# First attention: the products of probabilities and values issued for four steps at once in place of two

## Chip, cores, metric

One Trainium2 chip, one core in use. The metric is the time of the whole program on the device in microseconds (us), the median of several runs. The kernel before takes 1048.2 us, the median of 3 runs (1046.62 to 1052.95).

## What is computed

The program is a chain of cross-attention layers L0 to L3, each with its MLP, over 4 batches in float32. The change touches the attention of L0 alone, cut here to what matters (the queries come from 256 latent rows in each batch, the keys and values from 64 context rows joined with those 256 rows, 16 heads of 16):

```python
q = (latents @ q_w + q_b).reshape(b, 256, 16, 16)
kv = (concatenate([x, latents], axis=1) @ kv_w + kv_b).reshape(b, 320, 16, 16, 2)
kmat, v = kv[..., 0], kv[..., 1]
attn = einsum('bkhd,bnhd->bhkn', q, kmat) / 16
attn = softmax(where(mask, attn, -inf))
attn_out = einsum('bhkn,bnhd->bkhd', attn, v).reshape(b, 256, 256)
attn_out = attn_out @ out_w + out_b + latents
```

After it come an RMS norm and the MLP of L0, then the layers L1 to L3, which the change leaves alone.

## The kernel before

The first attention is `attend0` on PE (TensorE), with partner loops on ACT, DVE and POOL. It has N = 64 steps, one for each batch b (4), pair of heads r (8) and half u of the 256 query rows (2); `step0(n)` maps a step to them. Sixteen steps make one batch, called a block here, and "step s of a block" is i mod 16. The order on every engine is the written order of the loops, and each engine runs its own list; semaphores (`wait_ge`, `then_inc`) tie them together. There is no scheduler.

In iteration i of its loop PE issues, in this order: `scores(i)` (L592, two products of a head's queries and all keys, into one of two pairs of banks of `ps`); `spread(i + 4)` (L578, in even i also L581), which lays out keys or queries of a later pair of heads; `turn(i - 3)` (L603, five transposes of the normalised probabilities `prob0`, into banks 4 and 5 of `ps`, of which there is one set); in odd i from 5 on `values(i - 5)` (L616), for the steps i - 5 and i - 4. Each `values` call multiplies the 5 tiles of transposed probabilities `pT0` of its two steps with the values `V0`. `V0` has 32 columns, so the matmul uses a 128*32 part of the array, and the two steps of a call lie in different parts. After that come, in some steps of a block, extra work: `base` (L546, steps 8 and 12, projections of the next batch), `values_of` (L557, steps 10 and 14; L561 and L562, step 0) and `output` (L626, steps 4 and 6). A float32 matmul is two records in the trace, so the ten matmuls of a `values` call are the row "L616 x20".

The partners. DVE in iteration i: `max0(i)` (L1303, the row maximum of the scores, after `scores(i)`), `invert0(i - 1)` (L1318), in odd i `spread0(i + 4)` (L1295), in steps 9, 10, 13 and 14 `split0` (L1282 and L1284, SBUF to SBUF), and last `copy0(i - 3)` (L1309, the transposes out of `ps` into `pT0`, after `turn(i - 3)`). ACT: `spread0`, then `exp0(i)` (L1048) once the maximum is there, and `values0` (L1058) after every eighth step. POOL: the product of the probabilities with 1/sum (L441).

The two waits that the prediction follows are in `turn`: it waits for `pt0_ready`, that is for `copy0` of the step before, since the banks must be empty; and in `max0`, which waits for `scores`.

```python
pe.wait_ge(pt0_ready, n)              # turn(n): copy0(n - 1) is done
dve.wait_ge(s0_ps, n + 1)             # max0(n)
dve.wait_ge(t0_ps, n + 1)             # copy0(n)
```

Of the kernel before, what the change touches and what calls it, by code (L numbers as in the profile page):

```python
# [19 lines left out]
I32 = mybir.dt.int32  # L20
# [5 lines left out]
P = 128  # L26
D = 256
DH = D // P
B = 4
S = 256  # L30
C = 64
# [14 lines left out]
VT0 = 5  # L46
# [62 lines left out]
def build(nc, t):  # L109
    ctx = ExitStack()  # L110
    with ctx:
        def sb(name, shape, dt=F32):
            return ctx.enter_context(nc.sbuf_tensor(name, shape, dt))

        def sem(name):
            return ctx.enter_context(nc.semaphore(name))
# [8 lines left out]
        e16q = sb("e16q", [1, P])  # L125
        e48_f = sb("e48_f", [P, P])
        e48 = sb("e48", [P, P], F32R)
        mask_i = sb("mask_i", [P, B * C], I32)
        mask_u = sb("mask_u", [1, B * C], U8)
        mask_f = sb("mask_f", [P, B * C])  # L130
        mask0 = sb("mask0", [P, B * C], F32R)
        mask2 = sb("mask2", [1, B * C])
        arena = sb("arena", [P, 16384])
# [8 lines left out]
        V0 = arena[:, 5632:10752].rearrange("p (b t r c) -> p b t r c", b=B, t=VT0, r=PAIRS)  # L142
# [3 lines left out]
        prob0 = arena[:, 13824:13824 + 4 * 2 * KEYS0].rearrange("p (k n) -> p k n", k=4)  # L146

        copies_f = arena[:, 0:512].rearrange("p (w c n) -> p w c n", w=2, c=2)

        HL = sb("HL", [P, DH, 2, KEYS0 + S], F32R)  # L150

# [11 lines left out]
        u = sb("u", [P, 2, D])  # L163
# [22 lines left out]
        neg_half = sb("neg_half", [P, 2])  # L186
        sq = sb("sq", [P, D + 1])
        PN = H * C + H
        prob = sb("prob", [P, 2, PN])
        pT_all = sb("pT_all", [P, 4 * VT0 * P])  # L190
        pT = pT_all[:, 0:2 * 8 * P].rearrange("p (k c n) -> p k c n", k=2, c=8)
        pT0 = pT_all[:, :].rearrange("p (k c n) -> p k c n", k=4, c=VT0)
        mx = sb("mx", [P, 2, H])
        mx2 = sb("mx2", [P, 2, H])
        sm = sb("sm", [P, 2, H])
# [6 lines left out]
        ps = ctx.enter_context(nc.psum_tensor("ps", [P, 8, 512], F32))  # L202
# [27 lines left out]
        base_copied = sem("base_copied")  # L230
# [7 lines left out]
        pv0_ps = sem("pv0_ps")  # L238
# [4 lines left out]
        pt0_ready = sem("pt0_ready")  # L243
# [34 lines left out]
        rows_done = sem("rows_done")  # L278
# [18 lines left out]
        def col(name, i=0, n=1):  # L297
            at = COLS[name][0] + i
            return cols[:, at:at + n]
# [8 lines left out]
        def step0(n):  # L308

            quad, s = n // 4, n % 4  # L310
            return quad // 4, 2 * (quad % 4) + s % 2, s // 2
# [206 lines left out]
        def _(pe):  # L518
            mm = nc.tensor.matmul
# [18 lines left out]
            def attend0():  # L538
# [26 lines left out]
                def spread(n):  # L565

                    pair, w = n // 2, n % 2
                    b, r = pair // PAIRS, pair % PAIRS
                    m, j = r // 4, r % 4
                    cols_of = slice(KEYS0, KEYS0 + S) if w else slice(0, KEYS0)  # L570
                    width = S if w else KEYS0
                    if n >= 1:
                        pe.wait_ge(kq_ready, n)
                    if n >= 2 and w == 0:
                        pe.wait_ge(kq_dve, n // 2)
                    pe.wait_ge(hl_ready, 4 * b + 2 * m + w + 1)
                    for c in range(2):
                        last = mm(ps[:, 7, 0:width], copies[:, j, w, c, :], HL[:, m, c, cols_of],  # L578
                                  start=(c == 0), stop=(c == 1 and w == 1))
                    if w == 0:  # L580
                        last = mm(ps[:, 7, 0:C], e48[:, :], mask0[:, b * C:(b + 1) * C], start=False, stop=True)  # L581
                    last.then_inc(kq_ps, 1)

                def scores(n):
                    b, r, u = step0(n)
                    pair = b * PAIRS + r
                    pe.wait_ge(kq_ready, 2 * pair + 2)
                    pe.wait_ge(kq_dve, pair + 1)
                    if n >= 2:
                        pe.wait_ge(p0_ready, n - 1)  # L590
                    for e in range(2):
                        last = mm(ps[:, 2 * (n % 2) + e, 0:KEYS0], Q0[:, pair % 3, e, u * P:(u + 1) * P],  # L592
                                  K0[:, pair % 3, :], start=True, stop=True)
                    last.then_inc(s0_ps, 1)
# [11 lines left out]

                def values(n):

                    pe.wait_ge(pt0_ready, n + 2)
                    if n % 8 == 0 and n > 0:  # L610
                        pe.wait_ge(o0_ready, n // 8)
                    for c in range(VT0):
                        for i in (n, n + 1):
                            b, r, u = step0(i)
                            at = slice(32 * (r % 4), 32 * (r % 4) + 32)
                            last = mm(ps[at, 6, u * P:(u + 1) * P], V0[:, b, c, r, :], pT0[:, i % 4, c, :],  # L616
                                      start=(c == 0), stop=(c == VT0 - 1))
                    last.then_inc(pv0_ps, 1)

                def output(g):  # L620
# [19 lines left out]
                for i in range(N + 4):  # L640
                    step, b = i % 16, i // 16
                    if i < N:
                        scores(i)
                    if i + 4 < N:

                        if i == 1:
                            pe.wait_ge(base_copied, 3)
                        elif step in (9, 13) and b + 1 < B:
                            pe.wait_ge(base_copied, 4 * (b + 1) + (1 if step == 9 else 3))
                        spread(i + 4)  # L650
                    if 3 <= i < N + 3:
                        turn(i - 3)
                    if i >= 5 and i % 2 == 1:

                        if step == 1 and b < B:
                            pe.wait_ge(v0_ready, 3 * b + 3)
                        elif step in (5, 7) and b >= 1:
                            pe.wait_ge(rows_done, 2 * (b - 1) + (1 if step == 5 else 2))
                        elif step in (9, 13) and b + 1 < B:
                            pe.wait_ge(base_copied, 4 * (b + 1) + (2 if step == 9 else 4))  # L660
                        elif step in (11, 15) and b + 1 < B:
                            pe.wait_ge(v0_ready, 3 * (b + 1) + (1 if step == 11 else 2))
                        values(i - 5)

                    if i == 0 or step in (8, 12) and b + 1 < B:
                        if i == 8:
                            pe.wait_ge(in_kin, 16)
                        pe.wait_ge(kq_ready, i + 5)
                        base(2 if i == 0 else 4 * (b + 1) + (0 if step == 8 else 2))

                    if step == 0 and b < B:
                        if b == 0:
                            pe.wait_ge(base_copied, 2)
                        values_of(b, 2)
                    elif i == 2:
                        pe.wait_ge(v0_ready, 3)
                        base(3)
                    elif step in (4, 6) and 1 <= b < B:
                        output(2 * (b - 1) + (0 if step == 4 else 1))
                    elif step in (8, 12) and b + 1 < B:  # L680
                        if step == 12:
                            pe.wait_ge(o0_ready, 2 * b + 1)
                        base(4 * (b + 1) + (1 if step == 8 else 3))
                    elif step in (10, 14) and b + 1 < B:
                        values_of(b + 1, 0 if step == 10 else 1)
# [276 lines left out]

            pe.wait_ge(in_base, 32)
            attend0()
            mlp(0)
            keys(0, 0)
# [30 lines left out]
        def _(act):  # L997
# [54 lines left out]
            def values0(half):  # L1052

                b, d = half // 2, half % 2
                act.wait_ge(pv0_ps, 4 * (half + 1))
                if b >= 2 and d == 0:
                    act.wait_ge(o_ps, 2 * (b - 1))
                a_(oT0[:, b % 2, :, d, :], ps[:, 6, 0:2 * P].rearrange("p (u n) -> p u n", u=2), ACT.Identity,  # L1058
                   bias=col("L0_v_b", d)).then_inc(o0_ready, 1)
# [17 lines left out]
            for i in range(N + 4):  # L1077
                step, b = i % 16, i // 16
# [159 lines left out]
        def _(dve):  # L1238
            v = nc.vector
# [15 lines left out]
            for j in range(4):  # L1255
                last = v.tensor_scalar(copies[:, j, :, :, :], copies_f, col("strip", j), None, ALU.mult)
# [47 lines left out]

            def copy0(n):
                dve.wait_ge(t0_ps, n + 1)
                if n >= 4:
                    dve.wait_ge(pv0_ps, (n - 4) // 2 + 1)
                v.tensor_copy(pT0[:, n % 4, :, :].rearrange("p c n -> p (c n)"),  # L1309
                              ps[:, 4:6, :].rearrange("p q n -> p (q n)")[:, 0:VT0 * P]).then_inc(pt0_ready, 1)  # L1310

            def invert0(n):
# [16 lines left out]
            for i in range(N + 3):  # L1329
                step, b = i % 16, i // 16  # L1330
# [379 lines left out]
```

## Time and profile before

| what | value |
|---|---|
| median of 3 runs | 1048.2 us (1046.62 to 1052.95) |
| the profiled execution | 1048.33 us |
| its span, first to last instruction | 1046.5 us |
| mean granted TensorE clock | 0.983 |
| busy PE, PE weight loads, DVE, ACT, POOL | 958.0, 781.1, 631.1, 462.3, 344.7 us |

The profiled execution's own time is 1.8 us above its span. "Busy" counts the time in which an engine runs at least one instruction; it is an average over stages with different limits, and it doesn't say which engine sets the pace in the first attention. The granted clock is told in shares of 2.4 GHz, with 0.50 for 1.2 GHz.

### The profile page before, as it was taken

The page shows a single profiled execution, that of the slowest core. Times are in us where ns is not written, and L with a number is a line of the kernel's source. Part 1 is how long each engine was busy: PE and PEld are TensorE (multiplying, and loading weights), DVE is VectorE, ACT ScalarE, POOL GpSimd, SP SyncE. Part 2 cuts the span into 40 slices and gives each one's busy share as a digit, 9 for nine tenths or more (in the row PEclk, how much of TensorE's full clock was granted, in tenths as well). Part 3 has the DMA queues.
Part 4 walks back from the last instruction along what each step waited for, and adds up shares of the span by engine and source line. Part 5 has one row for each costly group of instructions (what it writes and reads, how often), then busy time and mean ns, then how long its engine had stood idle before and what let it go on. Part 6 is the DMA issues. An engine that isn't in the chain of part 4 may idle for free.

```text
span 1046.5 us, 15013 instructions
## 1 busy us (share of the span) xinstructions
PE 958.0 (92%) x5272; PEld 781.1 (75%) x5272; DVE 631.1 (60%) x1412; ACT 462.3 (44%) x1108; POOL 344.7 (33%) x382
## 2 busy tenths in 40 slices
PE   6789889799998999989799899799998989989898
PEld 4677778688895778856688688688885778756787
DVE  3788988611778847798611463511778847798410
ACT  3566667432564336633331342432673326633421
POOL 2644545410453325433321010110443335443210
PEclk8899999999999999999999998999999999999999
DMA  9100000000462004310000200200460004200000
GB/s 348 45 2 2 2 1 2 1 1 1 122 212 81 1 1 143 109 52 1 1 1 1 81 1 1 92 1 1 141 249 23 1 10 152 81 1 1 1 11 30
DMA packets 15020, 52.40 MB, mean 50 GB/s; under 512 B 1507, under 2 KB 4067, under 8 KB 13796
## 3 DMA queue, kind: packets, MB, share of 16 engines
q1 hardware_dynamic: 14948, 51.46, 14.4%
q8 instruction: 43, 0.70, 0.3%
q14 instruction: 29, 0.24, 0.1%
HBM read 50.41 MB, written 1.05 MB: 49 GB/s over the span
## 4 chain that ended last, share of the span: by engine, by line
PE 81%; DVE 11%; issue 3%; ACT 3%; POOL 1%; DMA 0%; SPq 0%; DVEq 0%; ACTq 0%
PE ps L947 11%; PE ps L771 10%; PE ps L795 9%; PE ps L934 9%; PE ps L698 5%; PE ps L700 5%; PE ps L738 5%; PE ps L727 4%; PE ps L616 4%; PE ps L603 3%; PE ps L783 2%; PE ps L592 2%; DVE pT_all L1309 2%; PE ps L841 2%; PE ps L546 1%
## 5 line engine op out<-in xcount | busy, mean ns | idle before, releaser
L771 PE MATMUL ps<-arena,hT 128*128 128x512 f32 x256 | 117.9, 604 | 15.0 <-ACT hT L1101 15.0
L795 PE MATMUL ps<-arena,pT_all 128*128 128x256 f32 x512 | 116.5, 381 | 7.5 <-ACT pT_all L1177 4.7
L1422 DVE TENSOR_TENSOR x<-ps,x 128x512 f32<-128x512 f32 x16 | 11.1, 692 | 183.9 <-PE ps L947 183.9
L934 PE MATMUL ps<-hT,w 128*128 128x256 f32 x512 | 114.8, 380 | 4.8 <-ACT hT L1120 4.8
L450 POOL TENSOR_TENSOR rstd<-var,neg_half 128x1 f32<-128x1 f32 (+1 forms) x56 | 36.4, 651 | 247.8 <-DVE var L1355 247.8
L947 PE MATMUL ps<-w,arena 128*128 128x256 f32 x512 | 113.3, 379 | 1.8 <-DVE x L1422 1.8
L441 POOL TENSOR_TENSOR arena<-arena,rinv 128x640 f32<-128x640 f32 x64 | 80.2, 1254 | 99.8 <-DVE rinv L1318 99.7
L795 PEld LDWEIGHTS ps<-arena,pT_all 128*128 128x128 f32 x512 | 94.7, 190 | 21.5 <-ACT pT_all L1177 5.7
L934 PEld LDWEIGHTS ps<-hT,w 128*128 128x128 f32 x512 | 96.0, 190 | 18.0 <-issue 5.6
L947 PEld LDWEIGHTS ps<-w,arena 128*128 128x128 f32 x512 | 97.1, 190 | 15.6 <-issue 2.5
L1131 ACT ACTIVATE arena<-ps,cols 128x256 f32<-128x256 f32 x128 | 53.6, 470 | 107.8 <-PE ps L934 107.8
L771 PEld LDWEIGHTS ps<-arena,hT 128*128 128x128 f32 x256 | 48.3, 192 | 65.7 <-issue 46.9
L469 POOL TENSOR_TENSOR prob<-prob,rinv 128x512 f32<-128x512 f32 x32 | 49.5, 1547 | 140.8 <-DVE rinv L1490 140.8
L1184 ACT ACTIVATE prob<-prob 128x512 f32<-128x512 f32 x32 | 20.2, 631 | 145.0 <-DVE prob L1480 145.0
L1048 ACT ACTIVATE arena<-ps,nb 128x320 f32<-128x320 f32 x128 | 66.3, 523 | 27.0 <-DVE nb L1303 24.9
L434 POOL TENSOR_TENSOR vacc<-vacc,vpart 128x256 f32<-128x256 f32 x60 | 44.1, 734 | 89.9 <-ACT vpart L1153 89.8
L1303 DVE TENSOR_REDUCE nb<-ps 128x2 f32<-128x640 f32 x64 | 52.4, 819 | 25.1 <-PE ps L592 25.0
L603 PE MATMUL ps<-ident,arena 128*128 128x128 f32 x320 | 47.9, 281 | 21.1 <-DVE pT_all L1309 21.0
L727 PE MATMUL ps<-HL,wq 128*128 128x256 f32 x384 | 67.2, 310 | 0.0
L425 POOL TENSOR_TENSOR u<-ring,lnb 128x256 f32<-128x256 f32 x64 | 66.3, 1036 | 0.0
L738 PE MATMUL ps<-ring,VT 128*128 128x256 f32 x256 | 66.0, 379 | 0.3 <-DVE x L1422 0.2
L700 PE MATMUL ps<-ctxT,ring 128*128 128x256 f32 x256 | 65.7, 379 | 0.0
(150 smaller groups left out, 1888.4 us busy)
## 6 DMA issues: line engine op xcount, KB each, us to landing
ring<-in_heads_dram SPq DMA_DIRECT2D x64, 512.5 KB, 3.6
w<-in_w_dram SPq DMA_DIRECT2D x8, 1024.0 KB, 7.3
x<-in_x_dram SPq DMA_DIRECT2D x1, 1024.0 KB, 10.2
lnb<-in_lnb_dram SPq DMA_DIRECT2D x4, 256.0 KB, 8.9
ring<-in_wp_dram SPq DMA_DIRECT2D x1, 1024.0 KB, 5.2
out_dram<-x SPq DMA_DIRECT2D x4, 256.0 KB, 2.1
arena<-in_kinT_dram SPq DMA_DIRECT2D x1, 960.0 KB, 7.5
brow<-in_brow_dram SPq DMA_DIRECT2D x1, 768.0 KB, 11.5
```

Source lines behind the costliest of these rows:

```text
L425: g.tensor_tensor(u[:, k, :], ring[:, n % RING, 512:768], scale, ALU.mult).then_inc(u_ready, 1)
L441: g.tensor_tensor(w, w, rinv[:, n % 2, 0:2].unsqueeze(2).broadcast_to([P, 2, KEYS0]), ALU.mult)\
L603: last = nc.tensor.transpose(ps[:, 4 + c // 4, (c % 4) * P:(c % 4 + 1) * P], prob0[:, n % 4, c * P:(c + 1) * P], ident[:, :])
L700: last = mm(ps[:, k, 256:512], w[:, 256 + d * P:256 + (d + 1) * P], ctxT[:, h % 2, d, :], start=(d == 0), stop=(d == 1))
L727: last = mm(ps[:, 2 + k, d * B * C:(d + 1) * B * C], wq[:, k, c, d * P:(d + 1) * P], KT[:, k, e, :], start=(p == 0), stop=(p == 2))
L738: last = mm(ps[:, 4 + k, g * D:(g + 1) * D], VT[:, k, g * P:(g + 1) * P], ring[:, n % RING, WO:WO + D], start=True, stop=True)
L771: last = mm(ps[:, half, :], hT[:, k, d, 0:P], A[:, d, b // 2, cols_of, sl, :].rearrange("p r s k -> p r (s k)"), start=(d == 0), stop=(d = ...
L795: last = mm(ps[:, 6, 0:D], pT[:, k, c, :], VW[:, b, c, :], start=(c == 0), stop=(c == PAIRS - 1))
L934: last = mm(ps[:, f // 2, (f % 2) * 256:(f % 2 + 1) * 256], w1[:, d, f * P:(f + 1) * P], hT[:, k, d, :], start=(d == 0), stop=(d == 1))
L947: last = mm(ps[:, 5 + u, 0:D], hid[:, k, f, u * P:(u + 1) * P], w2[:, f, :], start=(f == 0), stop=(f == FT - 1))
L1048: last = a_(prob0[:, n % 4, e * KEYS0:(e + 1) * KEYS0], ps[:, 2 * (n % 2) + e, 0:KEYS0], ACT.Exp, bias=nb[:, n % 2, e:e + 1], scale=-1.0, ...
L1131: a_(hid[:, b % 2, f, :], ps[:, f // 2, (f % 2) * 256:(f % 2 + 1) * 256], gelu, bias=col(bias, f)).then_inc(hid_ready, 1)
```

## The change

`values(n)` is now called in the iterations i = 7, 11, 15, ..., 67, for the steps i - 7 to i - 4, as two pairs in a row; before, it was called in every odd iteration from 5 on, for two steps. So a pair's products that stood in the steps 1, 5, 9 and 13 of a block stand two steps later, in front of those of steps 3, 7, 11 and 15. The transposed probabilities get eight slots in place of four, and the waits and counts follow (`pv0_ps` now counts groups of four). To make room in SBUF, `prob`, used by later stages, lies in `pT_all`, and `mask_i` and `mask_f`, used at the start, lie in `arena`; no instruction, size or order of theirs changes.

```diff
-        prob = sb("prob", [P, 2, PN])
-        pT_all = sb("pT_all", [P, 4 * VT0 * P])
+        pT_all = sb("pT_all", [P, 8 * VT0 * P])
+        prob = pT_all[:, 2 * 8 * P:2 * 8 * P + 2 * PN].rearrange("p (k n) -> p k n", k=2)
...
-        pT0 = pT_all[:, :].rearrange("p (k c n) -> p k c n", k=4, c=VT0)
+        pT0 = pT_all[:, :].rearrange("p (k c n) -> p k c n", k=8, c=VT0)
...
-                    pe.wait_ge(pt0_ready, n + 2)
+                    pe.wait_ge(pt0_ready, n + 4)
                     if n % 8 == 0 and n > 0:
                         pe.wait_ge(o0_ready, n // 8)
-                    for c in range(VT0):
-                        for i in (n, n + 1):
-                            b, r, u = step0(i)
-                            at = slice(32 * (r % 4), 32 * (r % 4) + 32)
-                            last = mm(ps[at, 6, u * P:(u + 1) * P], V0[:, b, c, r, :], pT0[:, i % 4, c, :],
-                                      start=(c == 0), stop=(c == VT0 - 1))
+                    for two in (n, n + 2):
+                        for c in range(VT0):
+                            for i in (two, two + 1):
+                                b, r, u = step0(i)
+                                at = slice(32 * (r % 4), 32 * (r % 4) + 32)
+                                last = mm(ps[at, 6, u * P:(u + 1) * P], V0[:, b, c, r, :], pT0[:, i % 8, c, :],
+                                          start=(c == 0), stop=(c == VT0 - 1))
                     last.then_inc(pv0_ps, 1)
...
-                    if i >= 5 and i % 2 == 1:
+                    if i >= 7 and i % 4 == 3:
 
-                        if step == 1 and b < B:
+                        if step == 3 and b < B:
                             pe.wait_ge(v0_ready, 3 * b + 3)
...
-                        values(i - 5)
+                        values(i - 7)
...
-                act.wait_ge(pv0_ps, 4 * (half + 1))
+                act.wait_ge(pv0_ps, 2 * (half + 1))
...
-                if n >= 4:
-                    dve.wait_ge(pv0_ps, (n - 4) // 2 + 1)
+                if n >= 8:
+                    dve.wait_ge(pv0_ps, (n - 8) // 4 + 1)
```

On PE, the steps 9 to 11 of the first block, where the trace of before waits most: `scores` is L592, `spread` L578 and L581, `turn` L603, `values` L616, `values_of` L557. Before:

```order
L592 MATMUL ps<-K,Q 128x320 x2
L578 MATMUL ps<-HL,copies 128x256 x2
L603 MATMUL ps<-ident,arena 128x128 x5
L616 MATMUL ps<-pT_all,arena 32x128 x10
L592 MATMUL ps<-K,Q 128x320 x2
L578 MATMUL ps<-HL,copies 128x320 x2
L581 MATMUL ps<-mask,e 128x64
L603 MATMUL ps<-ident,arena 128x128 x5
L557 MATMUL ps<-arena 128x128 x4
L592 MATMUL ps<-K,Q 128x320 x2
L578 MATMUL ps<-HL,copies 128x256 x2
L603 MATMUL ps<-ident,arena 128x128 x5
```

The same steps on PE in the changed kernel (its line numbers are higher by one or two, so `scores` is L593 and `values` L618), with the row that follows them:

```order
L593 MATMUL ps<-K,Q 128x320 x2
L579 MATMUL ps<-HL,copies 128x256 x2
L604 MATMUL ps<-ident,arena 128x128 x5
L593 MATMUL ps<-K,Q 128x320 x2
L579 MATMUL ps<-HL,copies 128x320 x2
L582 MATMUL ps<-mask,e 128x64
L604 MATMUL ps<-ident,arena 128x128 x5
L558 MATMUL ps<-arena 128x128 x4
L593 MATMUL ps<-K,Q 128x320 x2
L579 MATMUL ps<-HL,copies 128x256 x2
L604 MATMUL ps<-ident,arena 128x128 x5
L618 MATMUL ps<-pT_all,arena 32x128 x20
```

The ten products between the transposes of step 9 and the scores of step 10 are gone, and behind the transposes of step 11 stand twenty in place of ten. DVE, ACT and POOL keep their instructions and the order of these.

## Rows read from the trace of the kernel before

**Rows 1.** Windows: the first, second and fourth block; busy us of each engine, granted clock.

```profile
18.13:69.40 51.27, 41.12 (x306) 33.27 (x305) 38.17 (x65) 29.64 (x92) 24.40 (x23) 0.87 0.22 88
69.40:113.18 43.78, 38.99 (x362) 33.55 (x360) 37.47 (x67) 29.06 (x90) 20.05 (x17) 1.00 0.00 1
...
157.00:198.90 41.90, 36.41 (x375) 30.85 (x373) 34.21 (x67) 24.41 (x80) 21.54 (x19) 1.00 0.01 2
```

**Rows 2.** Waits of PE, 18 to 200 us: total us, times, longest us.

```profile
PE ps L603 <- DVE pT_all L1309: 21.0, 22, 2.1
```

**Rows 3.** Timeline of PE and DVE, steps 2 and 3 of the second block: start us, us.

```profile
73.87 0.56 PE L592 MATMUL ps<-K,Q 128*128 128x320 f32 x2
...
74.47 0.82 DVE L1303 TENSOR_REDUCE nb<-ps 128x2 f32<-128x640 f32 x1 [0.21 <-PE ps L592]
...
74.59 0.74 PE L603 MATMUL ps<-ident,arena 128*128 128x128 f32 x5
...
75.09 0.54 PE L592 MATMUL ps<-K,Q 128*128 128x320 f32 x2
...
75.41 0.80 DVE L1309 COPY pT_all<-ps 128x640 f32<-128x640 f32 x1
...
76.13 0.81 DVE L1303 TENSOR_REDUCE nb<-ps 128x2 f32<-128x640 f32 x1
...
76.36 0.74 PE L603 MATMUL ps<-ident,arena 128*128 128x128 f32 x5 [0.49 <-DVE pT_all L1309]
...
77.02 1.29 PE L616 MATMUL ps<-pT_all,arena 128*32 128x128 f32 x20
...
77.57 0.82 DVE L1309 COPY pT_all<-ps 128x640 f32<-128x640 f32 x1
...
78.24 0.56 PE L592 MATMUL ps<-K,Q 128*128 128x320 f32 x2
...
78.84 0.82 DVE L1303 TENSOR_REDUCE nb<-ps 128x2 f32<-128x640 f32 x1 [0.45 <-PE ps L592]
```

**Rows 4.** Timeline of PE from 77.38 us: what is left of that L616 group.

```profile
77.38 0.93 PE L616 MATMUL ps<-pT_all,arena 128*32 128x128 f32 x14
```

**Rows 5.** Timeline, steps 9 to 12 of the second block: PE, DVE and POOL.

```profile
91.96 1.29 PE L616 MATMUL ps<-pT_all,arena 128*32 128x128 f32 x20
92.26 1.25 POOL L441 TENSOR_TENSOR arena<-arena,rinv 128x640 f32<-128x640 f32 x1 [1.97 <-DVE rinv L1318]
...
92.74 0.96 DVE L1282 CAST HL<-arena 128x320 fp32r<-128x320 f32 x1
...
93.18 0.56 PE L592 MATMUL ps<-K,Q 128*128 128x320 f32 x2
...
93.87 0.19 PE L581 MATMUL ps<-mask,e 128*128 128x64 f32 x1
...
94.26 0.82 DVE L1309 COPY pT_all<-ps 128x640 f32<-128x640 f32 x1
...
95.23 0.74 PE L603 MATMUL ps<-ident,arena 128*128 128x128 f32 x5 [1.17 <-DVE pT_all L1309]
...
98.38 0.74 PE L603 MATMUL ps<-ident,arena 128*128 128x128 f32 x5 [0.98 <-DVE pT_all L1309]
```

**Rows 6.** Windows round the fall of the granted clock in the first block.

```profile
28.85:31.80 2.95, 1.09 (x6) 0.74 (x5) 2.45 (x7) 2.70 (x10) 2.59 (x3) 1.00 0.07 26
32.00:35.20 3.20, 1.50 (x7) 1.53 (x8) 2.49 (x5) 1.15 (x4) 2.04 (x3) 0.50 0.00 0
```

**Rows 7.** Timeline of PE, first block, steps 3 to 5, at the lower clock.

```profile
33.70 1.30 PE L603 MATMUL ps<-ident,arena 128*128 128x128 f32 x5 [2.09 <-DVE pT_all L1309]
34.65 0.88 PE L592 MATMUL ps<-K,Q 128*128 128x320 f32 x2
...
37.23 1.97 PE L616 MATMUL ps<-pT_all,arena 128*32 128x128 f32 x20
```

**Rows 8.** Timeline of PE, the last two turns and values of the attention.

```profile
194.68 1.29 PE L616 MATMUL ps<-pT_all,arena 128*32 128x128 f32 x20
195.89 0.77 PE L603 MATMUL ps<-ident,arena 128*128 128x128 f32 x5
197.57 1.29 PE L616 MATMUL ps<-pT_all,arena 128*32 128x128 f32 x20 [0.92 <-DVE pT_all L1309]
```

More of the change, by code:

```diff
@@ L127, in build @@
         e48 = sb("e48", [P, P], F32R)
-        mask_i = sb("mask_i", [P, B * C], I32)
         mask_u = sb("mask_u", [1, B * C], U8)
-        mask_f = sb("mask_f", [P, B * C])
         mask0 = sb("mask0", [P, B * C], F32R)
@@ L148, in build @@
         copies_f = arena[:, 0:512].rearrange("p (w c n) -> p w c n", w=2, c=2)
+        mask_i = arena[:, 512:768].bitcast(I32)
+        mask_f = arena[:, 768:1024]
         HL = sb("HL", [P, DH, 2, KEYS0 + S], F32R)
@@ L652, in attend0 @@
                         turn(i - 3)
-                    if i >= 5 and i % 2 == 1:
-                        if step == 1 and b < B:
+                    if i >= 7 and i % 4 == 3:
+                        if step == 3 and b < B:
                             pe.wait_ge(v0_ready, 3 * b + 3)
[L657 to L660, printed above, removed]
+                        elif step == 7 and b >= 1:
+                            pe.wait_ge(rows_done, 2 * b)
                         elif step in (11, 15) and b + 1 < B:
+                            pe.wait_ge(base_copied, 4 * (b + 1) + (2 if step == 11 else 4))
                             pe.wait_ge(v0_ready, 3 * (b + 1) + (1 if step == 11 else 2))
-                        values(i - 5)
+                        values(i - 7)
                     if i == 0 or step in (8, 12) and b + 1 < B:
@@ L1306, in copy0 @@
                 dve.wait_ge(t0_ps, n + 1)
-                if n >= 4:
-                    dve.wait_ge(pv0_ps, (n - 4) // 2 + 1)
-                v.tensor_copy(pT0[:, n % 4, :, :].rearrange("p c n -> p (c n)"),
+                if n >= 8:
+                    dve.wait_ge(pv0_ps, (n - 8) // 4 + 1)
+                v.tensor_copy(pT0[:, n % 8, :, :].rearrange("p c n -> p (c n)"),
                               ps[:, 4:6, :].rearrange("p q n -> p (q n)")[:, 0:VT0 * P]).then_inc(pt0_ready, 1)
```

## The prediction, made before the changed kernel had run

> **What bounds the kernel now.** I read first the windows of the blocks of sixteen steps [rows 1]: a full block takes 43.8 us (the third as well as the second), PE is busy for 39.0 of them and DVE for 37.5. Neither is clearly the bound; with two engines this close one has to ask who waits for whom, step by step. The waits of PE [rows 2] have one name in them: 22 times the transposes (L603, `turn`) wait for DVE's copy of the transposes of the step before (L1309), 21.0 us in all. So the banks of the transposes tie PE to DVE. The timeline of two neighbouring steps shows the loop [rows 3]. Even step: scores at 73.87, transposes at 74.59, next scores at 75.09, 1.22 us in all; PE is fast. Odd step: the scores have run ahead, but the transposes wait until 76.36, 0.15 after DVE's copy ends at 76.21; then come the values at 77.02, and the next scores at 78.24. DVE in turn starts its maximum 0.60 after the scores start (78.24 to 78.84) and had sat idle for 0.45. So PE waits for DVE in front of the odd transposes, and DVE waits for PE behind the odd values. In steps 9 to 12 [rows 5] both transposes wait, 1.17 and 0.98 us: DVE has the splits (L1282, L1284) in front of its copy.
>
> What matters for the change is where the values stand. Those at step 9 begin at 91.96 and are followed by scores at 93.18, and the transposes of step 10 begin only at 95.23, when DVE is ready. **The values of step 9 hide behind DVE; those of steps 3 and 11 stand behind a late transpose and in front of the scores, and hide behind nothing.** The change moves the first kind to the place of the second.
>
> **The price of a pair of steps in `values`.** The group is 20 records; 14 of them remain at 77.38 [rows 4], so six took 0.36 us, and the 14 take 0.79 up to the start of the last plus its own tail, some 0.057 each: 1.14 for twenty. From the start of the group to the next scores it is 1.22 (77.02 to 78.24), from transposes to values 0.66 (76.36 to 77.02) and from transposes straight to scores 0.50 (74.59 to 75.09). So a pair costs PE 0.66 + 1.22 - 0.50 = 1.38 where it stands alone, and 1.14 behind another. Sixteen joined groups save PE 16 x 0.24 = 3.8 us of its own time, which counts only where PE sets the pace.
>
> **Steps 9 to 12 and 13 to 16, six groups of four.** Without the values of step 9 the scores of step 10 come 1.38 earlier, at 91.80. That helps nobody: DVE's list up to the copy that ends at 95.08 (inversion, `spread0`, cast, difference, copy) rests on nothing that PE now does sooner. The cast at 92.74 takes 0.96 and ends 0.19 after POOL's product (92.26 + 1.25), and its place behind that product does not change. So the transposes stay at 95.23 and 98.38. Then come 40 records in place of 20: +1.14, uncovered. Six groups: 6 x 1.14 = **6.84**.
>
> **Plain groups of four.** Here DVE can recover something. I take two pairs like rows 3 and count from the first scores. Before: transposes 0.72 and 2.49, next scores 4.37, and the same again, 8.74 in all. After: the first transposes are the same; the second pair's scores come at 2.49 + 0.50 = 2.99. The copy that starts at 77.57 - 73.87 = 3.70 and takes 0.82 ends at 4.52, so the third transposes start at 4.67 (before 5.09). DVE's next maximum follows its copy by 0.72 (75.41 to 76.13), at 4.42; its copy follows that by 0.94 (74.47 to 75.41), at 5.36, but not before the transposes are done (0.82 after their start, 74.59 to 75.41), at 5.49; it ends at 6.29. Fourth transposes 6.44, values 7.10, next scores 7.10 + 1.22 + 1.14 = 9.46. That is +0.72: of 1.14 moved, 0.42 is caught up. The steps 0 to 3 and 4 to 7 of the last three blocks (six groups) hold extra PE work in even steps (L561, L626), so they lie between 0.72 and 1.14; taking the same recurrence through them with that work gives some 0.95: 6 x 0.95 = **5.7**. The one group without it (steps 8 to 11 of the last block): **0.72**. The next group has no `spread`, so DVE is shorter and catches up more: **0.45**.
>
> **The two ends.** First group, steps 4 to 7: the values of step 5 ran at 1.2 GHz for part of their 1.97 us [rows 7] and go to step 7, where the clock was 2.4 GHz; what is saved and what is added cancel, **+0.15**, from -0.5 to +2. Last group [rows 8]: the values at 194.68 stood where the next transposes followed at once, but each transposition there has a copy to wait for of 1.0 us, so little is gained; both pairs now come last, behind the last copy, with ACT's `values0`, the outputs and the norm waiting: **+1.14**.
>
> Edits at nothing: the new waits of `values`, for `pt0_ready` n + 4, ask for the same copy that `turn` of that iteration has already waited for; the `pv0_ps` wait of `copy0` asks for a group that was issued before and was never late; `prob`, `mask_i`, `mask_f` move in memory only. ACT's `values0` waits 1.14 longer in every eighth step, with nothing queued behind it that is due before PE's next step.
>
> **The sum.** 0.15 + 6.84 + 5.7 + 0.72 + 0.45 + 1.14 = **15.0 us**, for all sixteen joined groups. Bounds by the same rows: 16 x 0.72 = 11.5 and 16 x 1.14 = 18.2. All of it lies ahead of the L0 MLP, which can't begin before the last outputs, and the later stages only shift.
>
> **The granted clock** comes on top. It fell once in this attention: after 28.85, where PE was busy for 1.09 of 2.95 us, it went from 1.00 to 0.50, 1.2 GHz [rows 6]. The changed kernel makes a new hole: after step 10's mask matmul, which ended at 94.06 and now ends at 92.7, PE does nothing up to 95.23, 2.5 us in place of 1.17, six times over, and there are three waits of about 1.0 in a row at the end. At the lower clock the transposes take 1.30 for 0.74 and the scores 0.88 for 0.56 [rows 3, 7]; with the work of `values_of` and `spread` slowed alike, and the 0.98 of the next wait as cover, a fall costs about 1.3, and up to 3 if it reaches the joined values. I take three falls of 1.3, **4 us**; the ends are none (0) and seven of 3 (21).
>
> Against the profiled execution (1048.33, 0.1 from the median) that is 1048.2 + 15 + 4 = **1067**.
>
> **Rivals.** *Faster: PE is the bound.* If the 0.24 per joined group were gained in full and DVE followed, the time would be 1048.2 - 3.8 = 1044. For it: PE is the busiest engine. Against: PE's 22 waits in rows 2, and the values of step 9, which nobody waits for. A page speaks for this side: the Trainium skill, TensorEngine Tiling (Array Packing), Tiling Modes, Key Properties, says that changing the tiling mode drains TensorE, and the change halves the switches between 128*128 and 128*32. By that rule alone the result would be this rival's; the trace agrees that there is such a price, the 0.24 above. Chance 0.05.
>
> *No change.* DVE catches up all of it: it was idle for 0.21 and 0.45 in each plain pair [rows 3], so if its lists could be packed into 3.7 a pair the 1.14 would vanish, and 1048 stays. It needs the transposes' copy not to be tied to the turn before, which rows 5 contradict. Or the products of the second pair overlap with those of the first (other half of the bank), which takes 16 x 0.57 = 9.1 off and ends at 1054. Together 0.10.
>
> *Slower, with a clock that falls at nearly every hole:* 15 + 7 x 2 to 3, 1077 to 1084. Chance 0.15. *Slower, clock untouched:* 1063, chance 0.3. *The forecast:* 0.4.
>
> **The numbers.** Slower in all: 0.85. A measurement of this kernel can tell about 1%, 10.5 us; so slower by over 1% (over 1058.7) has 0.85, within 1% 0.10, faster 0.05. The range runs from 1057 (15 replaced by 11.5, with a little back from the start) to 1080 (the sum's upper end 18 and 14 for the clock) and leaves 0.2 out.
>
> **What the profile after would show.** Right: blocks two and three of 47.9 us or more in place of 43.8, with PE's and DVE's busy time nearly as before; waits of L604 for L1310 grown from 21 us to about 38; L618 as x40 rows of some 2.4 us; a DVE idle of 1.3 or so in front of the maximum behind each. In the clock row, a digit below 9 between 50 and 200 us for the added term. Wrong: a block under 44; x40 rows well under 2.3; transposes of step 10 that start sooner after the scores of step 8 than before.

## The result, and the profile after

The changed kernel takes 1067.47 us, the median of 4 runs (1066.49 to 1069.82), against 1048.23 (1046.62 to 1052.95). The ratio is 1.0176, with a 95% interval of 1.0143 to 1.0208: slower by 1.8%, where 1067 us had been forecast. The profiled execution took 1066.49 us, with a span of 1064.7 (before 1046.5). Five single runs far above the others of their kernel (two of the kernel before, three of kernels below, 1068.86 to 3741.94 us) are left out of every median and ratio.

Windows of the second and third block of the changed kernel, with the columns of [rows 1]:

```profile
70.88:118.96 48.08, 40.25 (x362) 35.29 (x361) 37.57 (x66) 29.16 (x90) 20.04 (x16) 0.96 0.01 2
118.96:166.92 47.96, 40.13 (x363) 35.16 (x361) 37.59 (x66) 29.17 (x90) 20.05 (x16) 0.96 0.01 1
```

A block that took 43.8 us [rows 1] takes 48.0. DVE, ACT and POOL do the work they did; PE's busy time grew by 1.2, and the mean clock is 0.96 in place of 1.00. So of the 4.2 us a block 3.0 are idle time of PE, and nearly all are idle time of DVE. PE's waits from 18 to 215 us name them in part:

```profile
PE ps L604 <- DVE pT_all L1310: 24.3, 26, 2.1
PE ps L579 <- issue: 6.1, 13, 0.5
```

The first line was 21.0 us [rows 2]; the second is new. Timeline of PE and DVE in steps 10 and 11 of the second block, to be read against [rows 5]:

```profile
95.08 0.54 PE L593 MATMUL ps<-K,Q 128*128 128x320 f32 x2
...
95.51 0.49 DVE L1296 TENSOR_SCALAR Q<-ps,cols 64x256 fp32r<-64x256 f32 x1
...
96.10 0.53 PE L579 MATMUL ps<-HL,copies 128*128 128x320 f32 x2 [0.48 <-issue]
96.47 0.19 PE L582 MATMUL ps<-mask,e 128*128 128x64 f32 x1
...
97.55 0.82 DVE L1310 COPY pT_all<-ps 128x640 f32<-128x640 f32 x1
...
98.52 1.30 PE L604 MATMUL ps<-ident,arena 128*128 128x128 f32 x5 [1.86 <-DVE pT_all L1310]
...
101.18 0.74 PE L593 MATMUL ps<-K,Q 128*128 128x320 f32 x2
...
102.00 0.71 PE L604 MATMUL ps<-ident,arena 128*128 128x128 f32 x5
...
102.64 2.38 PE L618 MATMUL ps<-pT_all,arena 128*32 128x128 f32 x40
```

The scores of step 10 now follow the transposes of step 9 at once, but the transposes start where they started before: 98.52, which is 4.62 us after the scores of step 9 (93.90), and before it was 95.23 - 90.61, also 4.62. The hole in PE is there in two pieces: 0.48 ahead of L579, which waits until DVE's L1296 has ended, and 1.86 behind the mask. The products then come as one run of 40 records, 2.38 us. The plain group of steps 8 to 11 of the last block:

```profile
186.66 0.56 PE L593 MATMUL ps<-K,Q 128*128 128x320 f32 x2
...
189.15 0.74 PE L604 MATMUL ps<-ident,arena 128*128 128x128 f32 x5 [0.49 <-DVE pT_all L1310]
...
191.33 0.74 PE L604 MATMUL ps<-ident,arena 128*128 128x128 f32 x5 [0.34 <-DVE pT_all L1310]
...
193.08 0.74 PE L604 MATMUL ps<-ident,arena 128*128 128x128 f32 x5 [0.48 <-DVE pT_all L1310]
193.75 2.38 PE L618 MATMUL ps<-pT_all,arena 128*32 128x128 f32 x40
...
196.05 0.56 PE L593 MATMUL ps<-K,Q 128*128 128x320 f32 x2
...
196.66 0.82 DVE L1304 TENSOR_REDUCE nb<-ps 128x2 f32<-128x640 f32 x1 [1.54 <-PE ps L593]
```

Counted from 186.66 the transposes start at 2.49, 4.67 and 6.42, and the next scores at 9.39; DVE has then been idle for 1.54 us, where it was 0.45 before [rows 3].

The granted clock, windows of the changed kernel round step 10 of the second block:

```profile
95.00:98.40 3.40, 1.18 (x8) 0.80 (x6) 3.27 (x7) 1.86 (x6) 1.25 (x1) 0.97 0.00 0
98.50:101.50 3.00, 2.98 (x14) 3.00 (x15) 2.96 (x5) 1.12 (x4) 1.25 (x1) 0.50 0.00 0
102.00:105.00 3.00, 3.00 (x48) 2.63 (x46) 2.17 (x4) 1.60 (x5) 1.25 (x1) 1.00 0.02 5
```

After a stretch in which PE was busy for 1.18 of 3.40 us the clock is 0.50, 1.2 GHz, and after one in which it was busy for 2.98 of 3.00 it is 1.00 again. It fell in four of the six holes (steps 10 and 14 of the first block, step 10 of the second and third), and twice at the end:

```profile
203.53 2.61 PE L618 MATMUL ps<-pT_all,arena 128*32 128x128 f32 x40
206.06 0.77 PE L604 MATMUL ps<-ident,arena 128*128 128x128 f32 x5
...
211.24 3.84 PE L618 MATMUL ps<-pT_all,arena 128*32 128x128 f32 x40 [0.92 <-DVE pT_all L1310]
```

The last products take 3.84 us for 2.38. The accounts by group of four steps, from one first scores (L593, or L592 before) to the next, in us; "split" groups hold DVE's splits:

| group | before | after | difference |
|---|---|---|---|
| first, steps 4 to 7 | 13.13 | 12.38 | -0.75 |
| split, six | 12.91 to 12.98 | 14.01 to 14.50 | +1.09 to +1.52, in all +7.75 |
| first of a block, three | 8.84 | 9.71 to 9.72 | +0.87 to +0.88 |
| second of a block, three | 9.10 | 10.03 | +0.93 |
| steps 8 to 11 of the last block | 8.73 | 9.39 | +0.66 |
| from step 12 of the last block to the MLP of L0 | 19.91 | 23.70 | +3.79 |

With -0.65 ahead of the first changed instruction these make 16.2 us at the start of that MLP. The other 2.0 us of the span appear later, in code that the change leaves alone: 3.1 more in L1's MLP and L2's attention, 1.2 less behind them.

### The profile page after: what moved, and what is told of

The parts are those of the page before. It is cut to its first block, busy times and chain, and to the rows that moved or that the text cites. A ratio compares the mean times of both kernels' runs of the same rounds, so it can differ in the third digit from the quotient of the medians.

```text
span 1064.7 us, 15003 instructions
## 1 busy us (share of the span) xinstructions
PE 964.1 (91%) x5272; PEld 789.4 (74%) x5272; DVE 632.0 (59%) x1412; ACT 462.6 (43%) x1108; POOL 344.6 (32%) x382
## 4 chain that ended last, share of the span: by engine, by line
PE 78%; DVE 13%; issue 4%; ACT 3%; POOL 1%; DMA 0%; SPq 0%; DVEq 0%; ACTq 0%
PE ps L948 10%; PE ps L796 9%; PE ps L772 9%; PE ps L935 9%; PE ps L699 5%; PE ps L701 5%; PE ps L739 5%; PE ps L728 4%; PE ps L618 4%; PE ps L604 3%; PE ps L784 2%; DVE pT_all L1310 2%; PE ps L842 2%; PE ps L859 2%; PE ps L547 1%
## 5 line engine op out<-in xcount | busy, mean ns | idle before, releaser
L470 POOL TENSOR_TENSOR pT_all<-pT_all,rinv 128x512 f32<-128x512 f32 x32 | 49.5, 1546 | 139.5 <-DVE rinv L1491 139.5
L1185 ACT ACTIVATE pT_all<-pT_all 128x512 f32<-128x512 f32 x32 | 20.2, 631 | 144.2 <-DVE pT_all L1481 144.2
L604 PE MATMUL ps<-ident,arena 128*128 128x128 f32 x320 | 50.4, 292 | 25.0 <-DVE pT_all L1310 24.3
```

The lines of the kernel that those rows point to most:

```text
L604: last = nc.tensor.transpose(ps[:, 4 + c // 4, (c % 4) * P:(c % 4 + 1) * P], prob0[:, n % 4, c * P:(c + 1) * P], ident[:, :])
```

## The experiments

Each ratio is to the kernel before on the same chip, in interleaved runs; its median in these was 1047.5 us (experiments 1 to 4), 1050.6 (5 and 7 to 9) and 1048.5 (6), so the ratios of two experiments compare better than their times. "MLP start" is the shift of the first MLP product against the trace of before; for the changed kernel it is +16.2.

**1. The memory alone.** Eight slots, and `prob`, `mask_i` and `mask_f` moved, with the schedule of before.

```diff
-                            last = mm(ps[at, 6, u * P:(u + 1) * P], V0[:, b, c, r, :], pT0[:, i % 4, c, :],
+                            last = mm(ps[at, 6, u * P:(u + 1) * P], V0[:, b, c, r, :], pT0[:, i % 8, c, :],
...
-                if n >= 4:
-                    dve.wait_ge(pv0_ps, (n - 4) // 2 + 1)
+                if n >= 8:
+                    dve.wait_ge(pv0_ps, (n - 8) // 2 + 1)
```

> The kernel before with the change's memory alone: eight slots of transposed probabilities, prob inside pT_all, mask_i and mask_f inside the arena; the products stay in pairs at every odd step. Theory P (place: products moved from steps where they lay beside DVE's work to steps where nothing covers them): 1048 us, blocks of 43.8 us. Rival M (the slots or the moved tensors cost something): 1055 or more. The other theories expect 1048 as well.

1047.90 us, the median of 9 runs, ratio 1.0008 (0.9982 to 1.0035). No trace of it is read here. The memory costs nothing that the times can tell, at most 0.35%; rival M falls.

**2. Never joined, one step later.**

```diff
-                    if i >= 5 and i % 2 == 1:
+                    if i >= 6 and i % 2 == 0:
...
-                        values(i - 5)
+                        values(i - 6)
...
-                    elif step in (4, 6) and 1 <= b < B:
-                        output(2 * (b - 1) + (0 if step == 4 else 1))
+                    elif step in (5, 7) and 1 <= b < B:
+                        output(2 * (b - 1) + (0 if step == 5 else 1))
```

> Eight slots, products in pairs and never joined, but each pair one step later, behind the transposes of the even steps (values(i - 6) in even i); outputs and their additions one step later too, so that no two of them meet in a bank. Theory P: the values of an even step push the next scores, so DVE's maximum and its copy come late and the next even transposes wait: a plain pair of steps goes from 4.37 to about 4.9 us, a block from 43.8 to about 50, the whole to 1064 to 1071 us although nothing is joined. Rival J (the cost of the change lies in the joining, in 40 records in a row): no loss, 1048 us. Rival D (fewer switches of the array's tiling matter): 1048, as it has as many as before.

1070.65 us, the median of 3 runs, ratio 1.0229 (1.0207 to 1.025), MLP start +18.8. Nothing is joined, and by both measures it is no faster than the changed kernel. A block of it:

```profile
71.96:120.47 48.51, 40.18 (x364) 33.71 (x362) 37.59 (x67) 29.55 (x91) 20.05 (x16) 1.00 0.01 2
```

and step 14 of the third block:

```profile
166.70 0.74 PE L604 MATMUL ps<-ident,arena 128*128 128x128 f32 x5 [1.86 <-DVE pT_all L1312]
...
167.37 1.29 PE L617 MATMUL ps<-pT_all,arena 128*32 128x128 f32 x20
```

The same wait of 1.86 stands in front of the transposes, and the products stand behind it. The clock was 1.00 in that block, so the 48.5 us are not the clock's. Rivals J and D fall: a loss of this size comes from the place, without joining and with as many switches of the tiling as before. It is spread otherwise than in the changed kernel, since every pair moved here: the first and second groups of a block take 10.40 and 10.57 us (9.72 and 10.03 in the changed kernel), the split ones without a fall of the clock 13.40 and 14.14 to 14.17.

**3. The first pair ahead of the transposes.**

```diff
+                        values(i - 7, 0)
                     if 3 <= i < N + 3:
                         turn(i - 3)
+                    if i >= 7 and i % 4 == 3:
+                        values(i - 7, 1)
```

> The changed kernel with the first pair of each group issued ahead of that step's transposes, where PE waits for DVE's copy, and the second behind them as before. Same steps, same groups of four. Theory P: the first pair lies in the wait of 0.5 to 1.0 us there, so a group costs 0.3 to 0.5 over before in place of 0.7 to 1.14: about 7 of the 15 us come back, less one more switch of tiling, 1055 to 1060 us; the hole in steps 10 and 14 stays. Rival J (a long run of products costs by its length): gone, 1048. Rival L (what costs is that a step holds two pairs at all, or the lag of seven steps): 1067, as the changed kernel.

1059.51 us, ratio 1.0128 (1.0094 to 1.0162), MLP start +9.6: 6.6 of 16.2 us come back there, and 5 by the ratios, where 7 were expected. A split group without a fall of the clock takes 13.17 us, 0.25 over before in place of 1.09, which is the bare rest of the pair behind the wait. Step 15 of the second block:

```profile
114.21 1.29 PE L618 MATMUL ps<-pT_all,arena 128*32 128x128 f32 x20
...
114.25 0.81 DVE L1313 COPY pT_all<-ps 128x640 f32<-128x640 f32 x1
...
115.42 0.77 PE L604 MATMUL ps<-ident,arena 128*128 128x128 f32 x5
...
116.12 1.28 PE L618 MATMUL ps<-pT_all,arena 128*32 128x128 f32 x20
```

The first pair starts while DVE still copies what the transposes wait for. But the second group of a block takes 10.36 to 10.38, more than the 10.03 of the changed kernel. There the transposes had not waited for DVE, so the pair in front only makes them late, and DVE sat idle for 0.75 ahead of their copy. Two of the six split groups had a fall of the clock in their hole, in step 10 of the second and third block, and take 14.62 and 14.72. The transposes behind it, in the second block:

```profile
97.43 1.30 PE L604 MATMUL ps<-ident,arena 128*128 128x128 f32 x5 [1.86 <-DVE pT_all L1313]
```

**4. DVE's copy ahead of its splits, in the changed kernel.**

```diff
+                early = step in (9, 10, 13, 14) and b + 1 < B
+                if early:
+                    copy0(i - 3)
                 if i == 1 or i == 3:
                     split0(2 if i == 1 else 3)
...
-                if i >= 3:
+                if i >= 3 and not early:
                     copy0(i - 3)
```

> The changed kernel with one edit on DVE: in steps 9, 10, 13 and 14 of the first three blocks the copy of the transposes stands ahead of the splits (L1283, L1285) in place of behind them. Theory P: the holes of PE in steps 10 and 14 came from that order and were what the values of steps 9 and 13 had filled; with the copy first they shrink, a block goes from 48.1 to about 45.1, in all 9 us less: 1056 to 1060 us, and the granted clock falls at fewer places. Rival: if DVE is full anyway, the splits only come back elsewhere and the time stays within 3 us of 1067.

1052.43 us, ratio 1.0054 (1.0036 to 1.0072), MLP start +2.6: 13.6 of 16.2 us come back there, 13 by the ratios, with no change of PE's list; 9 were expected. Its second block, and its waits from 18 to 200 us:

```profile
66.58:109.86 43.28, 39.00 (x363) 33.84 (x361) 35.42 (x67) 28.81 (x90) 20.05 (x17) 1.00 0.01 2
```

```profile
PE ps L604 <- DVE pT_all L1310: 15.5, 31, 2.1
```

A split group takes 11.75 to 11.82 us, less than the 12.92 of before. What I had missed is in DVE's column, 35.4 for 37.6 us. Steps 9 and 10 of the second block:

```profile
92.59 0.33 DVE L1283 CAST HL<-arena 128x320 fp32r<-128x320 f32 x1
...
94.33 1.25 POOL L442 TENSOR_TENSOR arena<-arena,rinv 128x640 f32<-128x640 f32 x1 [1.82 <-DVE rinv L1319]
...
94.89 0.85 DVE L1283 CAST HL<-arena 128x256 fp32r<-128x256 f32 x1
...
95.77 0.42 DVE L1285 TENSOR_TENSOR HL<-arena,HL 128x256 fp32r<-128x256 f32 x1
```

and the second split of before, step 10 of the same block:

```profile
95.80 0.27 DVE L1282 CAST HL<-arena 128x256 fp32r<-128x256 f32 x1
...
95.96 1.25 POOL L441 TENSOR_TENSOR arena<-arena,rinv 128x640 f32<-128x640 f32 x1 [2.45 <-DVE rinv L1318]
96.11 1.39 DVE L1284 TENSOR_TENSOR HL<-arena,HL 128x256 fp32r<-128x256 f32 x1
```

The difference takes 0.42 in place of 1.39 and the first cast 0.33 in place of 0.96, since neither runs beside POOL's product any more; the second cast now does, 0.85 for 0.27. In all it is 1.0 us less a group. That 13 us come back doesn't say that all of them were the change's cost: experiment 8 makes the same edit in the kernel before.

**5. and 6. The change in two halves.** Joined only in the six split groups, and joined only in the ten others; every pair signals by itself. In 6 the condition is the opposite.

```diff
+                        joined = (far % 16 in (11, 15) and b + 1 < B)
+                        if i % 4 == 3 or not joined:
...
+                            if joined:
+                                values(i - 7)
+                            values(i - 5)
```

> Eight slots; only the six groups at steps 9 to 12 and 13 to 16 of the first three blocks are joined (products of steps 9 and 13 moved to 11 and 15), all others stay in pairs at the odd steps, and every pair signals by itself. Theory P: 6 x 1.14 = 6.8 us, with a fall or three of the granted clock in the holes that this opens, 1 to 2 us: 1055 to 1058 us, and the plain parts of a block as before. If the cost of the change lay in the plain groups, 1048 to 1050.

> The counterpart of s_join_split: eight slots, the ten other groups joined (the products of steps 1 and 5 moved to 3 and 7, the last block and the ends), and the six groups round steps 9 to 16 of the first three blocks left in pairs. Theory P by the groups of the changed kernel's trace: +0.88 and +0.93 for the first two groups of three blocks, 5.4 in all, +0.66 for the next, -0.8 for the first one and 1.6 to 3.8 at the end: the attention ends 7 to 9 us later than before and the six groups keep 12.9 us; in all 1055 to 1059 us. The moves of s_join_split (8.2 us at the end of the attention) and of this one should add up to the change's 16.2.

Half 5 took 1061.51 us, ratio 1.0102 (1.0074 to 1.013), outside its expectation of 1055 to 1058; half 6 took 1057.38, ratio 1.0102 (1.0059 to 1.0145). In the first attention they did what was expected. In half 5 the split groups took 14.00 to 14.50 us and the others 8.83, 9.10 and 8.73, as before; the MLP starts at +8.2. In half 6 the split groups took 12.92 to 12.99 and the others 9.72, 10.04 and 9.39, as in the changed kernel; the MLP starts at +6.8, a little under the 7 to 9. The sum is 15.0 of the change's 16.2; what is missing lies at the end of half 6, from step 12 to the MLP 21.8 us for 23.7. Its values wait pair by pair, so that the last forty records start 0.9 us behind the transposes ahead of them and not 1.65, and its clock fell once there, not twice. The miss of half 5 lies behind the attention: its span is 14.1 us longer than that of before, 5.9 more than at the MLP start. Some of this is no effect of the edit, for the kernel before was slower in the same runs too, 1050.6 us. Half 6's traced execution is the fastest of its four (1050.56 us); its span is only 2.3 longer, 4.5 less than at the MLP start.

**7. The hole filled.** Six products that nobody reads, ahead of the transposes of steps 10 and 14.

```diff
+                def filler(i):
+                    pe.wait_ge(p0_ready, i)
+                    for _ in range(6):
+                        mm(ps[:, 2 * ((i + 1) % 2), 0:P], ident[:, :], ident[:, :], start=True, stop=True)
...
+                    if step in (10, 14) and b + 1 < B:
+                        filler(i)
```

> The changed kernel with six products more that nobody needs (identity by identity, into the scores' bank of the next step, which is free) in the hole of PE in steps 10 and 14 of the first three blocks, ahead of the transposes. Theory C (the granted clock falls in these holes and that costs time): the clock stays at 1.00 from 42 us to the last groups, and 2 to 4 us come back, 1063 to 1065 us. If the falls cost little, since the slower PE stands in front of another wait for DVE: within 1.5 us of 1067, with the clock at 1.00. If the products delay the transposes: slower, by up to 0.3 us a hole.

1065.51 us, ratio 1.0135 (1.0101 to 1.0169), MLP start +16.7. The windows from 60 to 200 us, of this kernel and then of the changed one:

```profile
60.00:200.00 140.00, 122.07 (x1129) 106.25 (x1127) 110.69 (x198) 86.06 (x269) 61.17 (x50) 1.00 0.01 1
```

```profile
60.00:200.00 140.00, 116.77 (x1064) 102.37 (x1062) 111.28 (x197) 85.83 (x268) 60.86 (x49) 0.96 0.01 1
```

PE does 5.3 us more and its clock no longer falls there. All six split groups take 14.01 to 14.08. In the changed kernel the two without a fall took 14.01 and 14.02, the four with one 14.19 to 14.50: a fall in a hole costs 0.2 to 0.5 us there, 0.3 on average, since the slower transposes stand in front of another wait for DVE. Experiment 3 shows the other side: there a pair of products fills that next wait, and a fall costs 1.45 and 1.55 us (14.62 and 14.72 for 13.17). The four falls in the holes of the changed kernel together cost 1.1 to 1.2 us. The times can't confirm it: the intervals of the two ratios overlap, and the MLP starts 0.5 us later, not sooner, since this execution was already 1.4 us later in step 4, ahead of anything that was changed.

**8. The copy first, in the kernel before.** The edit of experiment 4, with four slots and pairs at the odd steps.

> The kernel before, with four slots and pairs at the odd steps, and one edit on DVE: in steps 9, 10, 13 and 14 of the first three blocks the copy of the transposes stands ahead of the splits. In the changed kernel that edit took a group of steps 8 to 11 from 14.1 to 11.8 us, under the 12.9 of before. Theory P: here too PE's two waits of 1.17 and 0.98 us in such a group shrink to 0.2 to 0.3, six times: 5 to 8 us less, 1040 to 1043 us. Rival (the splits cost less only because the joined products gave them a quiet stretch of DVE): 1045 to 1048.

1042.18 us, the median of 6 runs (1039.86 to 1045.84), ratio 0.9921 (0.9895 to 0.9946), MLP start -8.2: faster than both kernels. Steps 10 and 11 of the second block, to be read against [rows 5]:

```profile
90.78 0.82 DVE L1309 COPY pT_all<-ps 128x640 f32<-128x640 f32 x1
91.22 0.56 PE L592 MATMUL ps<-K,Q 128*128 128x320 f32 x2
...
91.95 0.74 PE L603 MATMUL ps<-ident,arena 128*128 128x128 f32 x5
...
94.16 0.74 PE L603 MATMUL ps<-ident,arena 128*128 128x128 f32 x5
```

Neither of the two transposes waits; a split group takes 10.66 to 10.73 (steps 8 to 11) or 11.24 to 11.26 (steps 12 to 15) in place of 12.92. The first group of the next block gives back 0.8 (9.64 for 8.84), where DVE now runs behind. So the edit of experiment 4 is worth 8.2 us here and 13.6 in the changed kernel: only the difference, 5.4 us, give or take the microsecond by which the starts of two executions differ, is what DVE's order had added to the change's 16.2. Between the two kernels with the copy first the MLP start still moves by 10.8 us.

**9. Joined in the split groups, copy first.** Experiments 4 and 5 together.

> s_join_split with the copy ahead of the splits: joined groups only at steps 11 and 15 of the first three blocks, pairs elsewhere. The changed kernel with that copy order had 11.8 us for such a group against 12.9 before; pairs elsewhere cost as before. So 6 x 1.1 = 6.7 us under before: 1040 to 1043 us. Against s_before_copyfirst it says whether a joined group costs anything once the copy stands first: if the place alone counts, this one is 0 to 4 us slower than that.

1045.62 us, the median of 7 runs that lie far apart (1036.80 to 1049.42), ratio 0.9928 (0.9892 to 0.9964), MLP start -8.1. The median lies above the expected 1040 to 1043, while the ratio applied to the 1048.2 us of the kernel before gives 1040.7. Its split groups take 11.75 to 11.81 and the others 8.84 and 9.10, 41.4 a block against 40.7 in experiment 8. So each joined group still costs 0.4 us once the copy stands first; by the times the two kernels can't be told apart.

## Why the prediction was right, and where it wasn't

**The place.** The step that carried it was that the products of steps 9 and 13 lay beside DVE's splits and those of 11 and 15 beside nothing. The transposes of step 10 start 4.62 us after the scores of step 9 in both kernels, as forecast; experiments 2 and 3 show that the loss comes without joining and goes as far as a pair is put back into a wait. Part of it hangs on DVE's order: with the copy first in both kernels (experiments 4 and 8) the change costs 10.8 us of attention in place of 16.2, and a joined split group 0.4 (experiment 9) in place of 1.1.

**The terms.** Split groups: 1.14 each was forecast, 1.09 and 1.11 measured where the clock held. First and second groups of a block: 0.95, measured 0.88 and 0.93. The plain group: 0.72, measured 0.66, with the waypoints 4.67 and 6.44 against 4.67 and 6.42. These thirteen groups make 13.3 forecast and 12.7 measured, without the 1.1 that the falls of the clock cost in the split ones (7.75 - 1.14 + 5.42 + 0.66). The run of 40 records takes 2.38 us, the 1.29 of a pair and 1.09 for the second, where 1.14 was forecast; this small excess is most of the difference in the terms.

**The first group** was +0.15, from -0.5 to +2, and came at -0.75, below its range. One pair of traces can't size it: another -0.65 lies ahead of any changed instruction on PE, and over the traces of the experiments this group takes 11.79 to 12.67 us where it is joined and 12.39 to 13.13 where it is as before. So joining it gains some tenths, if anything, where the forecast had a small loss.

**The clock** was 4 us, as three falls of 1.3. The mechanism held, with four falls in the six holes and two at the end. The size was off at both places. In a hole it was 0.3 (experiment 7), because the next wait for DVE covers most of it; the 1.3 that was forecast holds where nothing covers it (experiment 3, 1.5). At the end the two falls cost 2.5: the last products take 3.84 for 2.38, and the transposes behind the first run of 40 start 10.01 us after the scores of step 12, against 8.96 in experiment 7, whose clock had not fallen by then. Together 3.7. So the 4 us came nearly right by two errors that cancel, twice the falls at half the price. Without the falls the last two groups cost 1.3 us, where 0.45 + 1.14 was forecast.

**The bounds of the waits.** I had expected 38 us for L604's waits on L1310; it was 24.3. A hole shows as two waits, of which one stands in the name of L579, and a slower PE is busy where a fast one waits. The blocks' length was the safe sign, the sum of one wait was not.

**What the total hides.** 15 + 4 gave 1067, and 1067.5 was measured. The mechanism was right, but agreement to half a microsecond is luck: the attention brought 16.2 in place of 19, and 2.0 more came from later stages, which the prediction had said would only shift. In the ten traces read here these stages take 838.5 to 849.0 us (843.0 before, 845.0 in the changed kernel), so those 2.0 can't be put down to the change. Of the rivals, "PE is the bound" falls with experiments 2 and 4: a joined group did save PE some of its own time, 0.29 us by the rows of the plain group (0.24 had been forecast), and that paid for nothing. "No change" falls with all of them: DVE catches up only 0.2 to 0.5 a group, in the groups without splits. Its second form, products that overlap, falls with the run of 40, whose second half takes 1.09 and not half of that. "A clock that falls at nearly every hole" was near in the number of falls, six, and wrong in their price.

Open: why the later stages took 5.9 us more in experiment 5 and 4.5 less in experiment 6. The granted clock goes along with it (below), but nothing was run that sets it.

## What to carry to other kernels

Before moving or merging work on an engine, look at what the engine would do at the old place: work that fills a wait for another engine is free there and costs most of its length, here 0.66 to 1.1 of 1.14 us, where nothing covers it, even if its own overhead falls. Where an engine's list holds one short step that another engine waits for behind long ones that nobody needs yet, exchange these first: here that gave 0.8% in the kernel before and 1.2% in the changed one. And before such an edit is read as the cause of a loss, make it in the kernel before as well.

## What the runs showed of the hardware

The stages behind the attention do the same work in every kernel here, and yet their length differs by some microseconds with the granted clock. Windows of before and of the changed kernel, from the middle of the program (the second attention of L1 has ended; L1's MLP, then L2's attention):

```profile
515.00:594.00 79.00, 70.78 (x329) 58.73 (x330) 23.76 (x54) 25.62 (x57) 14.91 (x18) 1.00 0.07 27
594.00:670.00 76.00, 67.04 (x432) 59.56 (x431) 38.48 (x74) 26.24 (x54) 7.55 (x11) 0.91 0.00 1
```

```profile
531.00:612.00 81.00, 72.52 (x329) 59.98 (x330) 23.98 (x55) 25.87 (x58) 14.89 (x18) 0.98 0.07 27
612.00:690.00 78.00, 68.36 (x433) 60.70 (x433) 39.42 (x78) 26.80 (x55) 7.59 (x12) 0.89 0.01 2
```

From its first product to that of the next stage the MLP takes 78.4 us before and 80.1 after, and L2's attention 76.7 and 78.1, with the same instructions, at a mean clock of 0.98 for 1.00 and of 0.89 for 0.91. Runs of the kernel before on one chip show it whole: 1047.22 us at a mean clock of 0.987, 1048.21 at 0.983, 1052.87 at 0.978 and 1054.66 at 0.977. Over the ten traces the time from the first MLP product of L0 to the end goes from 838.5 us (a mean clock of the whole run of 0.987) and 839.8 (0.990) to 849.0 (0.972) and 848.8 (0.969). Whether the clock makes the length, or idle time makes both, no run here separates. Differences of 5 us between single runs of this kernel are of that kind, so an edit worth less than this is better read from the length of its own stage than from the total.

The second finding is that DVE's SBUF-to-SBUF steps stretch beside POOL: the cast of 128x320 takes 0.33 us and 0.96, that of 128x256 0.27 and 0.85, the difference of 128x256 0.42 and 1.39. The stretched ones end 0.16 to 0.29 us after POOL's product. The Trainium skill, SBUF — State Buffer, section SBUF: two separate sides, says of the port pair that DVE and GpSimd share that the loser of it is blocked for the other's whole instruction; these rows agree in the main, though what is left behind POOL's product is 0.1 to 0.15 us less than the unstretched length. In experiment 4 it was worth some 2 us of DVE's time in a block.
